# Attention with key blocks in pairs, row maxima spread over the whole pass, and the divisions split between VectorE and GpSimd

## The chip, the cores and the metric

The kernel runs on one core of a Trainium2 chip. The metric is the device time of one execution in microseconds (us). It is one program of eight stages (four layers of a mixer and a feed-forward part each); the change touches one of them, the attention of the third layer.

## The reference, cut to attention

x is (4, 48, 48, 128), so each of 4 images is a sequence of 2304 tokens; there are 4 heads of 32 channels. Queries and keys are normalised over the sequence (axis 1), not over the channels.

```python
qkv = jnp.einsum('bxyc,cf->bxyf', x, w_qkv)
q, k, v = jnp.split(qkv, 3, axis=-1)          # each to (B, 2304, 4, 32)
q = l2norm_axis1(q)
k = l2norm_axis1(k)
sim = jnp.einsum('bihd,bjhd->bhij', q, k) * 10.0
attn = jax.nn.softmax(sim, axis=-1)
out = jnp.einsum('bhij,bjhd->bhid', attn, v)
out = jnp.einsum('bxyd,dc->bxyc', out, w_out) + b_out
```

## The kernel before

**Passes.** attention() works on pairs of heads. A pass, pair_of_heads(pair, build), attends with one pair and at the same time builds the next one: packs holds, for each of two pairs, queries and keys of both heads as three stacked groups of 32 rows (high and low parts of the numbers), and row 96 holds the negated row maximum of the scores, against a row of ones on the keys' side. So the score matmul gives score minus maximum, and Exp can be applied at once. There are nine passes in order: a bare one (pair None) that only builds, seven that attend and build, three of each kind inside a loop over the images, and a last one that only attends. project_heads (the projections to q, k and v) comes between some of them, output (the last matmul and the addition to x) between others. Every block of engine programs ends in a barrier of all engines.

**An attending pass.** The 2304 query columns are six chunks (NCH) of 384 (R_ORDER), the keys 18 blocks (NT_) of 128. For each of the 6 x 18 steps, score(j) (L2187) makes two matmuls, one a head, into one of two pairs of PSUM banks; ScalarE takes Exp of both into probs (three buffers, L2233); apply(j) (L2194) multiplies probs with v, in f32, the two heads into the two column halves of the array, and adds up in bank 4. v carries columns of ones, so that bank 4 also receives the sums of the weights. TensorE's order is apply(j), score(j+2), and a chunk's score(0) and score(1) come after the last apply of the chunk before. At a chunk's end ScalarE copies bank 4 to kept (L2237), and VectorE copies the sums to inv (L2266), inverts (L2268) and multiplies into OT (L2271).

**Building.** SyncE's queue issues 12 transfers from high and qk into packs (L2291) when the pass begins. From the second chunk on, TensorE's program has maxima matmuls (L2171) between the others, three a step in steps 2 to 17 of chunks 1 to 4 and in steps 2 to 9 of chunk 5. Each writes scores of 128 queries against 384 keys to one of banks 5 to 7, and VectorE reduces it to a column of top (L2251); the matmul waits until the bank's last reduce is done. There are 216 a pass. TensorE waits for all 12 transfers (semaphore packed) before the first maximum of each of these chunks. At the end top is reduced and negated (L2255), transposed by TensorE (L2175), copied (L2257), stored to DRAM and loaded into row 96 (L2293, L2295). In the bare pass the 216 maxima matmuls and reduces follow each other alone, over three banks.

**Before the first pass** GpSimd clears rows 96 to 127 of both halves of packs and sets the row of ones (L2016, L2019), while VectorE sets v's ones, neg and inv (L2009 to L2011).

Each engine works through its own program in the order written; nothing reorders it.

## Time and profile before

| | us |
|---|---|
| median of 3 runs (lowest, highest) | 10830.53 (10821.77, 10856.01) |
| profiled execution | 10839.46 |
| its span | 10837.6 |
| busy in the span: TensorE, VectorE, ScalarE, GpSimd | 8772.7, 7070.1, 4526.0, 4157.1 |

The profile is of one execution. Engines are PE (TensorE matmuls), PEld (its weight loads), DVE (VectorE), ACT (ScalarE), POOL (GpSimd) and SP (SyncE, which issues transfers); a q behind the name is the engine's queue. L2187 is line 2187 of the kernel. A row of the timeline merges equal instructions in a row: start in us from the span's start, length, line, operation, tiles, and xN for how many. An f32 product of two heads is four matmul records: the two heads beside each other, in two passes. A matmul's end is modelled, and consecutive matmuls overlap in the rows, so that distances between starts tell more than lengths. PEclk is the granted share of TensorE's clock: 1.00 is 2.4 GHz, 0.50 is 1.2 GHz. Attention lies between about 7976 and 9850 us of the span.

### The profile page before, as it was taken

Reading aid. Unit: us, or ns where it says so; the run is one execution under the profiler, and the core shown is the slowest. Engines: PE = TensorE matmul, PEld = TensorE weight load, DVE = VectorE, ACT = ScalarE, POOL = GpSimd, SP = SyncE. Lnnn points to the kernel's source line nnn. Section 1 sums busy time; section 2 is a strip of 40 time slices with the busy share of each in tenths; the row PEclk is TensorE's granted clock in tenths of the full one; section 3 lists DMA queues with packets and bytes.
Section 4 is the critical chain, followed back from the end, with each engine's and each line's share of the span. In section 5 each row is a group of like instructions: output and inputs, shape, how many; then the busy total and the mean of one; then the engine's idle time right before and its main releaser. Section 6 shows DMA issues by size and latency. Waiting matters only on the chain. (4 is left out here: it accounts for less than half of the span.)

```text
span 10837.6 us, 132369 instructions
## 1 busy us (share of the span) xinstructions
PE 8772.7 (81%) x41708; PEld 6246.0 (58%) x41708; DVE 7070.1 (65%) x9396; ACT 4526.0 (42%) x8541; POOL 4157.1 (38%) x2789
## 2 busy tenths in 40 slices
PE   5777777778777776799999999599748989896667
PEld 2444444444444443699999999588534444443445
DVE  6999899989988998444444444311256667653446
ACT  4666566656656665222222222122313444443231
POOL 3999599969977996111111111000000000000001
PEclk8999999999999998899999999766858999998678
DMA  4555355445544554000000000210310100003000
GB/s 130 165 161 164 111 162 163 144 129 161 162 131 144 160 163 128 16 14 12 14 10 14 14 12 10 76 35 21 125 37 22 24 18 14 21 11 126 16 25 18
DMA packets 332625, 835.00 MB, mean 77 GB/s; under 512 B 36307, under 2 KB 112247, under 8 KB 318301
## 3 DMA queue, kind: packets, MB, share of 16 engines
q1 hardware_dynamic: 331940, 826.57, 25.0%
q8 instruction: 345, 5.65, 0.2%
q14 instruction: 340, 2.78, 0.1%
HBM read 758.78 MB, written 39.08 MB: 74 GB/s over the span
## 5 line engine op out<-in xcount | busy, mean ns | idle before, releaser
L754 POOL TENSOR_TENSOR ss_work<-ss_dtu,ss_ringb 128x768 f32<-128x768 f32 x1536 | 2758.0, 1819 | 251.9 <-POOLq L59 248.5
L618 PE MATMUL ss_ps<-ss_work,ss_ident 128*128 128x512 f32 (+1 forms) x6144 | 2277.8, 517 | 446.4 <-POOL ss_work L764 327.4
L618 PEld LDWEIGHTS ss_ps<-ss_work,ss_ident 128*128 128x128 f32 x6144 | 1221.5, 203 | 1222.4 <-issue 877.7
L738 DVE TENSOR_TENSOR_SCAN ss_work<-ss_ps,ss_last,ss_work 128x768 f32<-128x768 f32 x1024 | 1811.4, 1802 | 96.0 <-issue 44.5
L671 ACT ACTIVATE ss_ps<-ss_dt,ss_a_neg 128x768 f32<-128x768 f32 x1536 | 1375.9, 896 | 273.1 <-DVE ss_work L738 254.6
L1234 ACT ACTIVATE stu_XT<-cv_ps 128x384 fp32r<-128x384 f32 x768 | 377.8, 492 | 1788.8 <-DVE cv_ps L1281 1361.4
L723 DVE TENSOR_TENSOR ss_work<-ss_work,ss_ps 128x1152 f32<-128x1152 f32 x768 | 1019.9, 1328 | 1.2 <-ACT ss_ps L679 1.2
L2233 ACT ACTIVATE at_probs<-at_ps 128x768 f32<-128x768 f32 x864 | 695.6, 811 | 705.6 <-PE at_ps L2187 705.0
L2251 DVE TENSOR_REDUCE at_top<-at_ps 128x1 f32<-128x384 f32 x1728 | 878.5, 553 | 164.7 <-PE at_ps L2171 163.1
L738 DVE TENSOR_TENSOR_SCAN ss_work<-ss_ps,ss_work 128x768 f32<-128x768 f32 x512 | 879.5, 1744 | 66.5 <-POOL ss_work L754 33.3
L1275 DVE TENSOR_TENSOR stu_XT<-cv_ps,stu_XT 128x384 fp32r<-128x384 f32 x768 | 428.4, 558 | 637.6 <-ACT stu_XT L1234 615.0
L1670 POOL MEMSET c_pooled<- 128x2048 f32 x2 | 3.6, 1808 | 2110.1 <-POOLq L59 2110.1
L764 POOL TENSOR_TENSOR ss_work<-ss_work,ss_ringc 128x384 f32<-128x384 f32 x768 | 771.5, 1005 | 85.8 <-DVE ss_work L738 66.5
L2194 PE MATMUL at_ps<-at_probs,at_v 128*64 128x384 f32 x3456 | 758.5, 517 | 31.0 <-ACT at_probs L2233 28.9
L1143 POOL TENSOR_TENSOR cv_near<-cv_raw,cv_one 128x768 fp32r<-128x768 f32 (+1 forms) x32 | 46.9, 1467 | 1896.4 <-PE cv_ps L1168 1888.3
L1168 PE MATMUL cv_ps<-cv_near,stu_u_high 128*128 128x384 f32 (+2 forms) x3072 | 634.9, 296 | 0.0
L2171 PE MATMUL at_ps<-at_packs 96*128 96x384 f32 x1728 | 576.6, 411 | 31.6 <-DMA at_packs<-at_high 31.6
L1185 PE MATMUL cv_ps<-stu_XT,cv_eff_high 128*128 128x144 f32 (+3 forms) x3072 | 577.4, 282 | 0.2 <-issue 0.2
L1281 DVE TENSOR_TENSOR cv_ps<-cv_ps,cv_shared 128x384 f32<-128x384 f32 x512 | 290.0, 566 | 414.6 <-PE cv_ps L1168 414.2
L2171 PEld LDWEIGHTS at_ps<-at_packs 96*128 96x128 f32 x1728 | 336.3, 200 | 377.2 <-DVE at_top L2251 324.5
L1271 DVE TENSOR_TENSOR stu_YT<-stu_YT,cv_ps 128x384 f32<-128x384 f32 x768 | 420.5, 548 | 181.6 <-PE cv_ps L1185 174.8
L2187 PE MATMUL at_ps<-at_packs 128*128 128x384 f32 x1728 | 482.3, 365 | 54.2 <-PEq L59 44.2
(546 smaller groups left out, 15466.7 us busy)
## 6 DMA issues: line engine op xcount, KB each, us to landing
ss_ringb<-scan_rows SPq DMA_DIRECT2D x768, 384.0 KB, 3.6
ss_ringc<-scan_rows SPq DMA_DIRECT2D x768, 384.0 KB, 3.7
c_w<-in_l_ffn_w SPq DMA_DIRECT2D x64, 1024.0 KB, 7.3
at_packs<-at_high SPq DMA_DIRECT2D x64, 288.0 KB, 5.5
cv_raw<-in_l_ffn_phi_odd SPq DMA_DIRECT2D x16, 576.5 KB, 3.7
cv_raw<-in_l_ffn_phi_even SPq DMA_DIRECT2D x16, 576.0 KB, 4.2
ffa_rows<-rows SPq DMA_DIRECT2D x16, 576.0 KB, 6.2
at_packs<-at_qk SPq DMA_DIRECT2D x32, 288.0 KB, 5.5
```

The source lines that it names most:

```text
L618: return pe.matmul(acc[:, d * WIN + a:d * WIN + e], ident[:, :], weighed[:, t % DEEP, d, a:e], start=n == 0 and e - a == 512, stop=n == NS ...
L671: act.activation(decay[d], dt[:, i % 2, d, :], ACT.Exp, scale=a_neg[:, SECTIONS[i][0], d, n:n + 1]).then_inc(s["decayed"], 1)
L723: dve.tensor_tensor(weighed[:, t % DEEP, :, 0:SPLIT], hid[:, t % DEEP, :, 0:SPLIT], bc(spread_c[:, None, :], [P, D2, SPLIT]), ALU.mult).th ...
L738: dve.tensor_tensor_scan(hid[:, t % DEEP, d, ::step], decay[d][:, ::step], drive[:, t % DEEP, d, ::step], start, ALU.mult, ALU.add).then_i ...
L754: pool.tensor_tensor(drive[:, t % DEEP, d, :], dtu[:, t // NST % 2, d, :], ringb[:, t % RING, :], ALU.mult).then_inc(s["driven"], 1)
L764: pool.tensor_tensor(weighed[:, t % DEEP, :, SPLIT:WIN], hid[:, t % DEEP, :, SPLIT:WIN], bc(ringc[:, t % RING, None, SPLIT:WIN], [P, D2, W ...
L1168: ins = pe.matmul(ps[:, bank, off:CW], blocks(a, g, parity), taps[kind][f][:, ::-1][:, from_:from_ + CW - off], start=start and g == 0 and ...
L1185: ins = pe.matmul(ps[:, 4 + c, lo:hi], (eff_high, eff_low)[a][:, kind, seg, :], (uk_high, uk_low)[f][:, (NCW * n + c) % SLOTS, lo:hi], sta ...
L2171: pe.matmul(ps_bank(ps, 5 + u % 3)[:, 0:R], packs[0:96, build, QUERIES, h, tile * P:(tile + 1) * P], packs[0:96, build, KEYS, h, u * R:(u ...
L2194: ins = pe.matmul(acc[64 * h:64 * h + 64, 0:R], v[:, j, 2 * pair + h, :, :].rearrange("p a d -> p (a d)"), probs[:, j % 3, h, :], start=j ...
L2233: act.activation(probs[:, j % 3, :, :], ps[:, 2 * (j % 2):2 * (j % 2) + 2, 0:R], ACT.Exp).then_inc(s["weighed"], 1)
L2251: dve.tensor_reduce(top[:, bass.ds(tile + h * NT_, 1), u], ps_bank(ps, 5 + u % 3)[:, 0:R], AX.X, ALU.max).then_inc(s["reduced"], 1)
```

## The change

probs has four buffers instead of three. TensorE goes through the 108 steps of a pass as 54 pairs, without regard to chunks: in pair p it makes the scores of steps 2p+2 and 2p+3 (of the next chunk too, where one ends), with the maxima that are due between them, and then the products of steps 2p and 2p+1. The maxima are in one list of 216, spread evenly over pairs 2 to 50 by maxima_due, four or five a pair; the wait for the 12 transfers stands before the first of them. ScalarE copies a chunk's result after the second exp of the next chunk. For the first five chunks GpSimd makes the copies of the sums and the multiplications, and VectorE the reciprocal in two halves, in two successive pairs; for the last chunk VectorE does all. In the bare pass the maxima are made in threes: three matmuls into three banks, one reduce over 3 x 384 columns, two sets of banks. The clearing of packs is split: VectorE does one half, GpSimd the other.

```diff
--- before.py
+++ after.py
@@ -1990,7 +1990,7 @@
-        probs = sb("probs", [P, 3, 2, R_ORDER])
+        probs = sb("probs", [P, 4, 2, R_ORDER])
@@ -1998,11 +1998,11 @@
-        xb = probs[:, :, :, :].rearrange("p a h r -> p (a h r)")
+        xb = probs[:, 0:3, :, :].rearrange("p a h r -> p (a h r)")
         ps = ctx.enter_context(nc.psum_tensor("at_ps", [P, 8, 512], F32))
-        c0 = Signals(nc, "at0", "cleared")
+        c0 = Signals(nc, "at0", "cleared filled")
         with nc.Block() as block:
             @block.vector
             def _(dve):
@@ -2010,18 +2010,20 @@
                 dve.memset(neg[:, :], 0.0)
                 dve.memset(inv[:, :], 1.0)
+                dve.memset(packs[96:P, 0, :, :, :].bitcast(F32), 0.0).then_inc(c0["cleared"], 1)
+                dve.wait_ge(c0["cleared"], 1)
+                dve.memset(packs[96:97, 0, KEYS, :, :].bitcast(F32), 1.0)
             @block.gpsimd
             def _(pool):
...
+                pool.memset(packs[96:P, 1, :, :, :].bitcast(F32), 0.0).then_inc(c0["filled"], 1)
+                pool.wait_ge(c0["filled"], 1)
+                pool.memset(packs[96:97, 1, KEYS, :, :].bitcast(F32), 1.0)
         c0.end()
         s1 = Signals(nc, "at1", "loaded made kept own squared rooted")
         s3 = Signals(nc, "at3", "packed mmade reduced negated turned copied stored placed "
-                                "scored weighed used kept divided own")
+                                "scored weighed used kept sums_ready inverted divided own")
@@ -2136,6 +2138,19 @@
+def maxima_groups():
+    return [(t, h, u) for t in range(NT_) for h in range(2) for u in range(NCH)]
+def maxima_due(p):
+    pairs = NCH * NT_ // 2
+    first, last = 2, pairs - 3
+    total = 2 * NT_ * NCH
+    return 0 if p < first else min(total, (p - first + 1) * total // (last - first))
 def pair_of_heads(nc, s, pair, build, vv):
@@ -2145,140 +2160,160 @@
     R = R_ORDER
     acc = ps_bank(ps, 4)
     STEPS = 2 * (len(ROWS[QUERIES]) + len(ROWS[KEYS]))
+    BLOCKS = NCH * NT_
+    GROUPS = maxima_groups()
...
+    def turned_sums(eng):
+        for h in range(2):
+            ins = eng.tensor_copy(inv[64 * h:64 * h + DH, :], kept[64 * h + DH:64 * h + 2 * DH, :])
+        return ins
+    def rows_of(c, h):
+        at = (2 * pair + h) * DH
+        return OT[at:at + DH, c * R:(c + 1) * R], kept[64 * h:64 * h + DH, :], inv[64 * h:64 * h + DH, :]
     with nc.Block() as block:
         @block.tensor
         def _(pe):
...
+            def maxima(g):
+                tile, h, u = GROUPS[g]
+                if g == 0:
+                    pe.wait_ge(s["packed"], 16 * STEPS)
+                at_least(pe, s["reduced"], g - 2)
+                pe.matmul(ps_bank(ps, 5 + g % 3)[:, 0:R], packs[0:96, build, QUERIES, h, tile * P:(tile + 1) * P],
+                          packs[0:96, build, KEYS, h, u * R:(u + 1) * R], start=True, stop=True).then_inc(s["mmade"], 1)
+            def maxima_of_three(g):
+                tile, h, u = GROUPS[3 * g]
+                at_least(pe, s["reduced"], g - 1)
+                for n in range(3):
+                    ins = pe.matmul(ps_bank(ps, 3 * (g % 2) + n)[:, 0:R], packs[0:96, build, QUERIES, h, tile * P:(tile + 1) * P],
+                                    packs[0:96, build, KEYS, h, (u + n) * R:(u + n + 1) * R], start=True, stop=True)
+                ins.then_inc(s["mmade"], 1)
...
+            def score(n):
+                c, j = n // NT_, n % NT_
+                at_least(pe, s["weighed"], n - 1)
+                for h in range(2):
+                    ins = pe.matmul(ps_bank(ps, 2 * (n % 2) + h)[:, 0:R], packs[:, pair, KEYS, h, j * P:(j + 1) * P],
+                                    packs[:, pair, QUERIES, h, c * R:(c + 1) * R], start=True, stop=True)
+                ins.then_inc(s["scored"], 1)
+            def apply(n):
+                c, j = n // NT_, n % NT_
+                pe.wait_ge(s["weighed"], n + 1)
+                if j == 0:
+                    at_least(pe, s["kept"], c)
+                for h in range(2):
+                    ins = pe.matmul(acc[64 * h:64 * h + 64, 0:R], v[:, j, 2 * pair + h, :, :].rearrange("p a d -> p (a d)"), probs[:, n % 4, h, :],
+                                    start=j == 0, stop=j == NT_ - 1, skip_group_check=True)
+                ins.then_inc(s["used"], 1)
+            if pair is None:
+                pe.wait_ge(s["packed"], 16 * STEPS)
+                for g in range(len(GROUPS) // 3):
+                    maxima_of_three(g)
+                turn()
+            else:
                 score(0)
                 score(1)
...
+                for p in range(BLOCKS // 2):
+                    due = range(maxima_due(p - 1), maxima_due(p)) if build is not None else []
+                    for g in due[0:2]:
+                        maxima(g)
+                    if p + 1 < BLOCKS // 2:
+                        score(2 * p + 2)
+                    for g in due[2:3]:
+                        maxima(g)
+                    if p + 1 < BLOCKS // 2:
+                        score(2 * p + 3)
+                    for g in due[3:]:
+                        maxima(g)
+                    apply(2 * p)
+                    apply(2 * p + 1)
+                    if build is not None and p == BLOCKS // 2 - 3:
                         turn()
...
         @block.scalar
         def _(act):
...
+            def weigh(n):
+                act.wait_ge(s["scored"], n + 1)
+                at_least(act, s["used"], n - 3)
+                act.activation(probs[:, n % 4, :, :], ps[:, 2 * (n % 2):2 * (n % 2) + 2, 0:R], ACT.Exp).then_inc(s["weighed"], 1)
+            def keep(c):
+                act.wait_ge(s["used"], (c + 1) * NT_)
                 at_least(act, s["divided"], c)
                 act.activation(kept[:, :], acc[:, 0:R], ACT.Copy).then_inc(s["kept"], 1)
             if pair is not None:
-                chunks(act, weigh)
+                for n in range(BLOCKS):
+                    weigh(n)
+                    if n > NT_ and n % NT_ == 1:
+                        keep(n // NT_ - 1)
+                keep(NCH - 1)
         @block.vector
         def _(dve):
...
+            def reduce(g):
+                tile, h, u = GROUPS[g]
                 dve.wait_ge(s["mmade"], g + 1)
...
+                dve.tensor_reduce(top[:, bass.ds(tile + h * NT_, 1), u], ps_bank(ps, 5 + g % 3)[:, 0:R], AX.X, ALU.max).then_inc(s["reduced"], 1)
+            def reduce_three(g):
+                tile, h, u = GROUPS[3 * g]
+                dve.wait_ge(s["mmade"], g + 1)
+                dve.tensor_reduce(top[:, bass.ds(tile + h * NT_, 1), u // 3], ps[:, 3 * (g % 2):3 * (g % 2) + 3, 0:R], AX.XY, ALU.max).then_inc(s["reduced"], 1)
+            def negate(parts):
+                dve.wait_ge(s["reduced"], 2 * NT_ * parts)
+                dve.tensor_reduce(neg[:, 0:2 * NT_], top[:, :, 0:parts], AX.X, ALU.max, negate=True).then_inc(s["negated"], 1)
                 dve.wait_ge(s["turned"], 1)
                 dve.tensor_copy(topT[:, :].bitcast(F32R), ps_bank(ps, 5)[:, 0:P]).then_inc(s["copied"], 1)
...
+            def half_inverted(c, half):
+                dve.wait_ge(s["sums_ready"], c + 1)
+                part = inv[:, half * R // 2:(half + 1) * R // 2]
+                dve.reciprocal(part, part).then_inc(s["inverted"], 1)
+            if pair is None:
+                for g in range(len(GROUPS) // 3):
+                    reduce_three(g)
+                negate(NCH // 3)
+            else:
+                for p in range(BLOCKS // 2):
+                    for g in range(maxima_due(p - 1), maxima_due(p)) if build is not None else []:
+                        reduce(g)
+                    if p >= NT_ // 2 and p % (NT_ // 2) in (1, 2):
+                        half_inverted(p // (NT_ // 2) - 1, p % (NT_ // 2) - 1)
+                if build is not None:
+                    negate(NCH)
+                ch = Chain(dve, s["own"])
+                dve.wait_ge(s["kept"], NCH)
+                ch.link(turned_sums(dve))
                 ch.link(dve.reciprocal(inv[:, :], inv[:, :]))
                 for h in range(2):
-                    at = (2 * pair + h) * DH
-                    ins = dve.tensor_tensor(OT[at:at + DH, c * R:(c + 1) * R], kept[64 * h:64 * h + DH, :], inv[64 * h:64 * h + DH, :], ALU.mult)
+                    ins = dve.tensor_tensor(*rows_of(NCH - 1, h), ALU.mult)
                 ins.then_inc(s["divided"], 1)
+        @block.gpsimd
+        def _(pool):
             if pair is not None:
...
+                for c in range(NCH - 1):
+                    pool.wait_ge(s["kept"], c + 1)
+                    turned_sums(pool).then_inc(s["sums_ready"], 1)
+                    pool.wait_ge(s["inverted"], 2 * (c + 1))
                     for h in range(2):
...
+                        ins = pool.tensor_tensor(*rows_of(c, h), ALU.mult)
+                    ins.then_inc(s["divided"], 1)
         @block.sync
         def _(sp):
```

## Rows read from the trace of the kernel before

**Rows 1.** The page, costliest groups: busy and mean | idle before, and its releaser
```profile
L2171 PE MATMUL at_ps<-at_packs 96*128 96x384 f32 x1728 | 576.6, 411 | 31.6 <-DMA at_packs<-at_high 31.6
```

**Rows 2.** Windows: stretch, length, busy us of PE, PEld, DVE, ACT, POOL; PEclk, DMA, GB/s
```profile
7982.30:8006.30 24.00, 0.00 (x0) 0.00 (x0) 2.50 (x3) 0.00 (x0) 23.30 (x4) 0.50 0.00 0
...
8057.50:8158.80 101.30, 100.50 (x216) 62.03 (x216) 100.46 (x217) 0.00 (x0) 0.00 (x0) 0.50 0.00 0
8165.90:8356.40 190.50, 186.53 (x865) 92.95 (x865) 133.61 (x243) 90.67 (x115) 0.00 (x0) 0.98 0.09 20
...
8359.60:8368.30 8.70, 0.00 (x0) 0.00 (x0) 1.68 (x3) 0.00 (x0) 0.00 (x0) 0.50 0.39 136
8393.60:8400.40 6.80, 6.28 (x16) 2.73 (x16) 0.00 (x0) 3.59 (x4) 0.00 (x0) 0.50 0.86 174
...
9673.00:9823.70 150.70, 146.60 (x648) 54.72 (x648) 21.78 (x25) 89.39 (x113) 0.00 (x0) 0.99 0.00 1
```

**Rows 3.** Timeline, TensorE, a block without maxima: start, us, engine, line, operation
```profile
8181.24 0.61 PE L2187 MATMUL at_ps<-at_packs 128*128 128x384 f32 x2
8181.78 0.87 PE L2194 MATMUL at_ps<-at_probs,at_v 128*64 128x384 f32 x4
```

**Rows 4.** Timeline, a block with three maxima, TensorE and then VectorE
```profile
8240.11 0.87 PE L2194 MATMUL at_ps<-at_probs,at_v 128*64 128x384 f32 x4
8240.91 0.44 PE L2171 MATMUL at_ps<-at_packs 96*128 96x384 f32 x1
8241.19 0.52 PE L2187 MATMUL at_ps<-at_packs 128*128 128x384 f32 x2
8241.54 0.52 PE L2171 MATMUL at_ps<-at_packs 96*128 96x384 f32 x2
8241.99 0.87 PE L2194 MATMUL at_ps<-at_probs,at_v 128*64 128x384 f32 x4
...
8241.39 1.55 DVE L2251 TENSOR_REDUCE at_top<-at_ps 128x1 f32<-128x384 f32 x3 [0.32 <-PE at_ps L2171]
```

**Rows 5.** Timeline of TensorE, the first instructions of the first attending pass
```profile
8165.92 1.62 PE L2187 MATMUL at_ps<-at_packs 128*128 128x384 f32 x4 [6.24 <-PEq L59]
8167.97 1.55 PE L2194 MATMUL at_ps<-at_probs,at_v 128*64 128x384 f32 x4 [0.43 <-ACT at_probs L2233]
8169.45 1.01 PE L2187 MATMUL at_ps<-at_packs 128*128 128x384 f32 x2
```

**Rows 6.** DMA issues (page: last column us to landing), SyncE and ScalarE at two passes
```profile
at_packs<-at_high SPq DMA_DIRECT2D x64, 288.0 KB, 5.5
...
8179.77 1.41 SPq L2291 DMA_DIRECT2D at_packs<-at_high  x1
...
8356.35 0.49 ACT L2237 ACTIVATE at_kept<-at_ps 128x384 f32<-128x384 f32 x1 [0.96 <-PE at_ps L2194]
...
8614.64 1.40 SPq L2291 DMA_DIRECT2D at_packs<-at_high  x1
...
8795.59 0.49 ACT L2237 ACTIVATE at_kept<-at_ps 128x384 f32<-128x384 f32 x1 [0.96 <-PE at_ps L2194]
```

**Rows 7.** Timeline at a chunk's end, TensorE
```profile
8225.76 0.95 PE L2171 MATMUL at_ps<-at_packs 96*128 96x384 f32 x3
```

**Rows 8.** Reciprocals of VectorE by line, busy us and mean ns
```profile
L2268 DVE RECIPROCAL at_inv<-at_inv 128x384 f32<-128x384 f32 x6 | 15.3, 2553 | 0.2
...
L111 DVE RECIPROCAL at_ln_rstd<-at_ln_std 128x72 f32<-128x72 f32 x1 | 0.6, 603 | 0.4 <-ACT at_ln_std L121 0.4
```

**Rows 9.** Operations of another stage, from the page
```profile
L764 POOL TENSOR_TENSOR ss_work<-ss_work,ss_ringc 128x384 f32<-128x384 f32 x768 | 771.5, 1005 | 85.8 <-DVE ss_work L738 66.5
...
L723 DVE TENSOR_TENSOR ss_work<-ss_work,ss_ps 128x1152 f32<-128x1152 f32 x768 | 1019.9, 1328 | 1.2 <-ACT ss_ps L679 1.2
```

**Rows 10.** Memsets of GpSimd and of VectorE by line
```profile
L2016 POOL MEMSET at_packs<- 32x9216 f32 x2 | 15.5, 7773 | 273.5 <-POOLq L59 273.5
...
L320 DVE MEMSET ss_dtr<- 32x2304 f32 x1 | 2.0, 1978 | 0.5 <-issue 0.5
```

More of the change, by code:

```diff
@@ L2166, in _ @@
         def _(pe):
-            def maxima(group):
-                g, tile, h, u = group
-                pe.wait_ge(s["reduced"], g + 1)
-                pe.matmul(ps_bank(ps, 5 + u % 3)[:, 0:R], packs[0:96, build, QUERIES, h, tile * P:(tile + 1) * P], packs[0:96, build, KEYS, h, u * R:(u + 1) * R], start=True, stop=True).then_inc(s["mmade"], 1)
+            def maxima(g):
[12 more added lines that the diff above has]
+                ins.then_inc(s["mmade"], 1)
             def turn():
@@ L2198, in attend @@
+            if pair is None:
[4 more added lines that the diff above has]
+            else:
                 score(0)
                 score(1)
-                at_least(pe, s["kept"], c)
-                for j in range(NT_):
-                    apply(j)
-                    at = 3 * (j - 2)
-                    for group in groups[at:at + 1] if j >= 2 else []:
-                        maxima(group)
-                    if j + 2 < NT_:
-                        score(j + 2)
-                    for group in groups[at + 1:at + 3] if j >= 2 else []:
-                        maxima(group)
-                    if build is not None and c == NCH - 1 and j == 12:
-                        turn()
@@ L2215, in _ @@
-            if pair is not None:
-                chunks(pe, attend)
-            else:
-                pe.wait_ge(s["packed"], 16 * STEPS)
-                for tile in range(NT_):
-                    for h in range(2):
-                        for u in range(NCH):
-                            maxima(((2 * tile + h) * NCH + u, tile, h, u))
-                turn()
+                for p in range(BLOCKS // 2):
[13 more added lines that the diff above has]
+                    if build is not None and p == BLOCKS // 2 - 3:
+                        turn()
@@ L2239, in _ @@
             if pair is not None:
-                chunks(act, weigh)
+                for n in range(BLOCKS):
[3 more added lines that the diff above has]
+                keep(NCH - 1)
         @block.vector
         def _(dve):
-            ch = Chain(dve, s["own"])
-            dve.sem_inc(s["reduced"], 3)
-            def reduce(group):
-                g, tile, h, u = group
+            def reduce(g):
+                tile, h, u = GROUPS[g]
@@ L2256, in negate @@
                 dve.wait_ge(s["turned"], 1)
                 dve.tensor_copy(topT[:, :].bitcast(F32R), ps_bank(ps, 5)[:, 0:P]).then_inc(s["copied"], 1)
-            def divide(c):
-                for group in maxima_groups(c):
-                    reduce(group)
-                if build is not None and c == NCH - 1:
-                    negate()
-                dve.wait_ge(s["kept"], c + 1)
-                for h in range(2):
-                    ins = dve.tensor_copy(inv[64 * h:64 * h + DH, :], kept[64 * h + DH:64 * h + 2 * DH, :])
-                ch.link(ins)
+            def half_inverted(c, half):
+                dve.wait_ge(s["sums_ready"], c + 1)
+                part = inv[:, half * R // 2:(half + 1) * R // 2]
+                dve.reciprocal(part, part).then_inc(s["inverted"], 1)
@@ L2268, in divide @@
                 ch.link(dve.reciprocal(inv[:, :], inv[:, :]))
                 for h in range(2):
-                    at = (2 * pair + h) * DH
-                    ins = dve.tensor_tensor(OT[at:at + DH, c * R:(c + 1) * R], kept[64 * h:64 * h + DH, :], inv[64 * h:64 * h + DH, :], ALU.mult)
+                    ins = dve.tensor_tensor(*rows_of(NCH - 1, h), ALU.mult)
                 ins.then_inc(s["divided"], 1)
+        @block.gpsimd
+        def _(pool):
             if pair is not None:
-                chunks(dve, divide)
-            else:
-                for tile in range(NT_):
+                for c in range(NCH - 1):
+                    pool.wait_ge(s["kept"], c + 1)
+                    turned_sums(pool).then_inc(s["sums_ready"], 1)
+                    pool.wait_ge(s["inverted"], 2 * (c + 1))
@@ L2278, in _ @@
                     for h in range(2):
-                        for u in range(NCH):
-                            reduce(((2 * tile + h) * NCH + u, tile, h, u))
-                negate()
+                        ins = pool.tensor_tensor(*rows_of(c, h), ALU.mult)
+                    ins.then_inc(s["divided"], 1)
         @block.sync
```

41 lines of the change are left out of this document (removed).

## The prediction

> **What bounds the kernel now.** I read the page first, then busy time and clock by stretch, then the attention passes instruction by instruction, and last the transfers that feed them. It puts the weight of the kernel elsewhere: attention takes some 1850 of 10,838 us, and nothing outside it is edited. So only attention is worked out. On the page, see one line: the maxima matmuls waited 31.6 us for a transfer into at_packs [rows 1]. That is the first, bare pass, the only place where maxima are asked for as soon as a pass begins.
>
> By stretch [rows 2], an attending pass that also builds the next pair's maxima is 190.5 us long with TensorE busy in 186.5, VectorE in 133.6 and ScalarE in 90.7; the last pass, which builds nothing, has 146.6 of 150.7. TensorE bounds both. In the bare pass VectorE is busy 100.5 of 101.3 us, and TensorE stands at 0.50 of its clock (1.2 GHz).
>
> The steps show what TensorE's time is made of. Without maxima [rows 3] a block is two score matmuls and four product records (two heads side by side, two passes each), and repeats every 1.34 us: the scores start 0.54 us before the products, and the products 0.80 after that give way to scores. With three maxima [rows 4] it is 1.87 us from one product start to the next (8240.11 to 8241.99, with the rounding of a row). Narrow matmuls in a row start 0.177 apart (8241.19 to 8241.54 is two of them). A second product pass starts 0.87 - 0.49 = 0.37 us after the first. With these, a block of 2 scores and a product would be 2 x 0.177 + 2 x 0.373 = 1.10; it takes 1.34. So 0.24 us is paid for changing over from scores to products and back, and the same 0.24 is left with five narrow matmuls: 1.87 - 5 x 0.177 - 0.746. No exp is late: ScalarE is idle for half of the pass.
>
> **Pairs of blocks.** 108 blocks a pass become 54 pairs, each 4 x 0.177 + 4 x 0.373 + 0.24 = 2.44 us without maxima. One changeover in two goes: 54 x 0.24 = 13.0 us a pass. What no row shows is a product right behind another block's product. Low end 0.373 a pass, as inside a block; high end a full drain, which by the score row and the latest product end is about 0.2 us each, 54 x 0.2 = 11 us a pass. I take the low one, since the second pass inside a block writes the same bank with new weights and pays 0.373. The Trainium skill, "TensorEngine Tiling (Array Packing)", Tiling Modes, says that the array drains when its tiling mode changes, not when only the tile does. Two products share one mode; by that rule the low end holds and the rival of a drain below loses weight; the 0.24 above agrees with it.
>
> **Next chunk's scores ahead.** Now the first product of a chunk waits for kept, behind the last product and a 0.49 copy. A building pass of 72 x 1.87 + 36 x 1.34 = 182.9 takes 190.5; the last 108 x 1.34 = 144.7 takes 150.7. The rest, 7.6 and 6.0, is five chunk ends and the start at the low clock. In the new order four scores (0.8 us with the changeover) stand between a chunk's last product and the next one, and the copy begins 0.05 us after the product and takes 0.5: hidden, with 0.2 to spare. With four probs buffers neither exp nor product waits: a pair's two exps are 1.6 us in 2.44.
>
> Last pass: start at the low clock and first pair 5.3 us (four score matmuls 1.6 us, a wait for exp, four more, and a product at 1.48 for 0.80 until the clock rises [rows 5]), then 52 pairs x 2.44 = 126.9, the last without scores 1.5: 133.7 against 150.7. **Gain 17.0 us.**
>
> **Maxima spread over the pass: the wait.** The seven building passes ask for maxima from the third pair (maxima_due is 0 for p below 2, then about 4.4 a pair to p = 50). The first of them still waits for all 12 transfers into packs, and TensorE's queue holds everything behind it: scores, products, hence ScalarE and VectorE. Third pair begins at 5.3 + 2.4 and a little, 8 to 9 us after TensorE's start. SyncE issues the last transfer at 8179.77, the pass having begun at 8165.92 [rows 5, 6], and such a transfer lands 5.5 us after its issue: 19.4 us in. Now that is hidden, as no maximum is asked for in the first chunk (26 us long). **TensorE will stand still for about 11 us**; in the two passes behind output, where SyncE starts 3.5 us before TensorE, for 7.
>
> So a building pass is best counted from that landing to its end. Before: 8185.3 to the last copy's start at 8356.35, 171.1, in the pass shown; 175.5 in the third (last issue 8614.64, copy 8795.59) [rows 6]. Of the seven, four are of the first kind (171.4 mean), two of the second (175.4), and the seventh is 169.0: 1205.4 us together. After, by terms:
> - 49 pairs x 2.44 and 216 maxima x 0.177: 157.8.
> - two pairs without maxima 4.9, the last pair 1.5, the turn 0.2: 6.6.
> - Bank waits. Three banks take the maxima. A reduce starts 0.38 after its matmul, the next 0.47 behind it, it ends after 0.55, and a matmul held by it starts 0.15 after that end [rows 4, 7] (three in a row take 0.95 us where 0.80 is due, as the last was held for its bank). In a pair with five maxima (216 - 4 x 49 = 20 of them) the fifth is wanted at 8 x 0.177 = 1.42 and its bank is free at 0.38 + 0.47 + 0.55 + 0.15 = 1.55: 20 x 0.14 = 2.8.
> - Half reciprocals. The rows for 384 and 72 columns, 2553 and 603 ns [rows 8], give 1.35 us for 192. Two pairs in each of five chunks have it behind their reduces. Worked pair by pair it makes the next pair's maxima wait 0.2 to 0.5: 2.7 in all. Bounds: nothing, if the backlog is gone by the next pair; 0.5 each, 5.
> - Clock. From 3.2 us after a pass's end the clock was 0.50 with TensorE idle; a restarted TensorE had 0.50 for 6.8 us in the second pass [rows 2], and 4 to 8 in the others. The stall is long enough for that. At the low clock a product goes by in 1.48 for 0.80 (8167.97 to 8169.45), and four score matmuls take 1.62 for 0.97 [rows 5], so 5.5 us of it lose 2.4.
> Sum 172.3, times seven 1206.1, against 1205.4. **Gain 0.** Without the transfer wait a pass would be 5.3 + 2.4 + 157.8 + 6.6 + 5.5 = 177.6 against 190.5: the spreading takes back what pairs bring.
>
> Behind it: the last product to the pass's end (copy, turn, reciprocal, multiply of the last chunk) stays on VectorE, as now. The turn comes 4 us before the last product instead of 6; the two small transfers behind it need 3.6, and VectorE's tail is 5, so they stay covered.
>
> **Division shared with GpSimd.** GpSimd is idle here [rows 2]; its two copies of 32x384 have no row; a 128x384 two-input op of its own is 1.0 us [rows 9], which I take as the upper end, nothing as the lower. They start when kept is done, and VectorE asks for the result a pair later, 4.8 us on. Hidden; the copies may cost 2.4 us each before TensorE feels it. The multiplies have a chunk's time.
>
> **Bare pass in threes of banks.** 72 reduces of 1152 columns. 216 now take 100.5, 0.465 each, of which successive ones overlap by 0.09. VectorE's 1152 columns with a PSUM input take 1.33 in another stage [rows 9], so 1.24 each, 89.3 in all. But two sets of three banks go round a ring: three matmuls with their handshakes, at the low clock 1.43 (1.62 for four less one spacing of 0.32, and 0.13 for the waits), then the reduce, 1.33, for two groups: 1.38 a group, 99.4. The clock was 0.50 through 101 us of this pass [rows 2] with one matmul in 0.465; the new pass would be as dense. I take 1 us gained; 11 if the clock rises.
>
> **Memsets.** GpSimd's four take 23.3 of the 24.0 us before the first loads [rows 2, 10]. Split: VectorE has its 2.5 and 9216 columns at the 1.98 per 2304 of its own row, 7.9, and half of that, 4.0: 14.5. Gain 8.2 (bounds 11.6, GpSimd's own half, and 0 if they share a port). The Trainium skill, "GPSIMD Engine Reference", Key points, warns that GpSimd and a VectorE instruction in a two-port mode contend for memory. Here VectorE's three memsets (2304, 384 and 128 columns) took 2.50 us beside GpSimd's [rows 2], against 2.42 at the rate of the lone one at L320 [rows 10]; the trace speaks against a loss. By that rule, if it held for memsets, the 8.2 would shrink towards 0.
>
> **Sum.** 17.0 - 0.7 (called 0 above) + 1 + 8.2, about 25.5 us. The profiled execution took 10,839.5 (its span 10,837.6 and 1.9 around it), 0.08% over the median 10,830.5 of the runs; I put the difference on the median: 10,805, 0.24% less. A measurement here can tell about 0.3% (32 us).
>
> **Rivals.**
> 1. VectorE's backlog is harmless: no bank or reciprocal wait, 7 x 5.5 = 38 us, perhaps the clock of the bare pass too (10): 10,757 to 10,790, I say 10,780. For it: VectorE is busy for 70% only. Against: a row in which the fourth matmul was held [rows 7].
> 2. The transfers don't hold the third pair. Then 7 x (190.5 - 177.6) = 90 more: 10,715. Nothing speaks for it but that landings could come earlier; the wait is on all twelve.
> 3. **Slower:** a product drains before the next block's product. 0.2 us at 54 places in 8 passes, 86 us: 10,891. For: no row shows the seam. It decides from 0.06 us a seam, where the gain is gone. Against: the second pass in a block.
> 4. VectorE's queue is worse than worked: contention of GpSimd's copies with its reduces, or reciprocals in pairs of five that each hold TensorE 1 us instead of 0.3: 7 x 10 x 0.7 = 49: 10,854.
>
> **How the numbers follow.** Forecast 0.52 (own range 10,788 to 10,828), rival 1 0.20, rival 2 0.07, rival 3 0.09, rival 4 0.12. Faster by over 0.3% is below 10,798: rivals 1 and 2 nearly whole, 0.26, and 0.11 of the forecast's: 0.37. Slower, above 10,863: rival 3 and 0.03 of rival 4: 0.12. Within: 0.51. The range 10,770 to 10,855 leaves out rivals 2 and 3 and the edges of 1 and 4.
>
> **What would show it.** TensorE idle for 7 to 11 us at the first maxima matmul in each building pass, released by a transfer into at_packs, then about 6 us at 0.50 of the clock; pairs of 2.44 us in the last pass, 3.15 and 3.46 with four and five maxima; building passes again near 190, the last 134; the bare pass near 100 at clock 0.50; GpSimd's memsets 11.7 us. Building passes near 178 would refute the wait; pairs of 2.6 or more the changeover.

## The result and the profile after

| | before | after |
|---|---|---|
| median (lowest to highest), us | 10836.2 (10821.8 to 10856.0), 4 runs | 10750.5 (10737.0 to 10765.3), 4 runs |
| ratio | | 0.9919, 95% interval 0.9905 to 0.9934 |
| span of the profiled execution, us | 10837.6 | 10753.0 |

The change makes the kernel 0.8% faster, some 86 us. I had forecast 25 us, within the noise, and a range down to 10,770: the time lies outside it, on the fast side.

The page of the kernel after, its span, busy TensorE, and the line that answers to [rows 1]. Columns of the last: busy, mean ns | idle before it.

```profile
span 10753.0 us, 132231 instructions
PE 8643.1 (80%) x41708; PEld 6312.2 (59%) x41708; DVE 6950.3 (65%) x9134; ACT 4479.2 (42%) x8541; POOL 4262.7 (40%) x2947
...
L2187 PE MATMUL at_ps<-at_packs 96*128 96x384 f32 x1512 | 497.6, 376 | 63.0 <-DMA at_packs<-at_high 62.9
```

The maxima matmuls of the seven building passes now wait 62.9 us for a transfer in all: about 10 us (9.9 to 10.7) in five of them and 6.0 in the two behind output. Before, they waited for none. The 31.6 us of [rows 1] was the bare pass's own wait; after the change that matmul stands at another line (L2194), its wait is as long as it was, and it is not in the 62.9.

Windows of the kernel after, columns as in [rows 2]: the clearing of packs, the bare pass, the first attending pass and, within it, the stall and what follows, and the last pass.

```profile
7977.00:7994.80 17.80, 0.00 (x0) 0.00 (x0) 14.13 (x5) 0.00 (x0) 11.70 (x2) 0.50 0.00 0
8046.90:8148.20 101.30, 93.05 (x216) 59.20 (x216) 94.49 (x73) 0.00 (x0) 0.00 (x0) 0.50 0.00 0
8155.10:8338.50 183.40, 172.51 (x865) 102.29 (x865) 116.84 (x228) 85.40 (x114) 14.95 (x20) 0.96 0.10 20
8163.90:8174.20 10.30, 0.01 (x1) 0.00 (x0) 0.00 (x0) 0.00 (x0) 0.00 (x0) 0.71 0.91 187
8174.30:8178.40 4.10, 4.10 (x12) 2.92 (x14) 2.14 (x4) 1.62 (x2) 0.00 (x0) 0.50 0.00 0
9610.60:9740.80 130.20, 129.89 (x648) 62.98 (x648) 12.82 (x10) 84.13 (x113) 14.91 (x20) 0.97 0.00 1
```

The first building pass is 183.4 us instead of 190.5, the last pass 130.2 instead of 150.7, and the bare pass as long as before at the same 0.50 of the clock. From first score to last product, the seven building passes together went from 1333.8 to 1279.5 us (54.3 less), the last from 150.7 to 130.2 (20.5), the clearing from 23.4 to 17.7 (5.7), the bare pass with its tail from 108.3 to 108.3. The gaps between passes took 2.7 more, which I can't explain, and 5.3 us of the difference of the two spans lie before attention, where nothing was edited: variation between executions.

TensorE at the third pair of the first attending pass (timeline: start, us, line, operation, count, idle before and its releaser):

```profile
8162.77 1.14 PE L2216 MATMUL at_ps<-at_probs,at_v 128*64 128x384 f32 x6
8174.27 1.01 PE L2187 MATMUL at_ps<-at_packs 96*128 96x384 f32 x2 [10.37 <-DMA at_packs<-at_high]
```

That is the forecast stall: 10.37 us, released by the last transfer into at_packs. It stands in every building pass: in the five where TensorE and SyncE start together the landing is 19.0 to 19.3 us after TensorE's first score, in the two behind output 15.3. The window from 8163.9 shows no engine busy, with the transfers at 0.91 of the DMA engines, and the one from 8174.3 has TensorE at 0.50 for 4.1 us. All that was close to the forecast (11 us and 7 us of standing still, then 5.5 us at the low clock). What was not is the pair itself. TensorE in the last pass:

```profile
9650.50 0.97 PE L2206 MATMUL at_ps<-at_packs 128*128 128x384 f32 x4
9651.40 1.51 PE L2216 MATMUL at_ps<-at_probs,at_v 128*64 128x384 f32 x8
9652.84 0.97 PE L2206 MATMUL at_ps<-at_packs 128*128 128x384 f32 x4
9653.74 0.87 PE L2216 MATMUL at_ps<-at_probs,at_v 128*64 128x384 f32 x4
```

Compare [rows 3]. Two products follow each other in 1.51 us; the first pass of the run is 0.373 as before, and (1.51 - 0.49 - 0.37) / 2 = 0.32 separates the later ones. From scores to scores it is 1.44 us for two products, against 2 x 0.80. The whole pair repeats every 2.34 us (9650.50 to 9652.84, or 9651.40 to 9653.74), where I had 2.44.

A pair with five maxima, TensorE and then VectorE:

```profile
8229.90 0.62 PE L2187 MATMUL at_ps<-at_packs 96*128 96x384 f32 x2
8230.36 0.52 PE L2206 MATMUL at_ps<-at_packs 128*128 128x384 f32 x2
8230.72 0.34 PE L2187 MATMUL at_ps<-at_packs 96*128 96x384 f32 x1
8230.90 0.51 PE L2206 MATMUL at_ps<-at_packs 128*128 128x384 f32 x2
8231.25 0.65 PE L2187 MATMUL at_ps<-at_packs 96*128 96x384 f32 x2
8231.83 1.51 PE L2216 MATMUL at_ps<-at_probs,at_v 128*64 128x384 f32 x8
8233.27 0.62 PE L2187 MATMUL at_ps<-at_packs 96*128 96x384 f32 x2
```

```profile
8230.38 2.42 DVE L2269 TENSOR_REDUCE at_top<-at_ps 128x1 f32<-128x384 f32 x5 [1.10 <-PE at_ps L2187]
8232.72 1.34 DVE L2285 RECIPROCAL at_inv<-at_inv 128x192 f32<-128x192 f32 x1
8233.97 1.88 DVE L2269 TENSOR_REDUCE at_top<-at_ps 128x1 f32<-128x384 f32 x4
```

Such a pair is 3.37 us (8229.90 to 8233.27), one with four is 3.05: the fifth costs 0.32, its own 0.177 and 0.14 of waiting for its bank, as worked. Behind it VectorE's half reciprocal of 1.34 us delays the next pair's first reduce by 0.22, and the four matmuls of that pair don't notice (8233.27 to 8236.34, 3.07).

### The profile page after: what moved, and what is told of

Same layout as the page of the kernel before. It is cut to its first block and busy times, and to the rows that moved or that the text cites. A ratio compares the mean times of both kernels' runs of the same rounds, so it can differ in the third digit from the quotient of the medians.

```text
span 10753.0 us, 132231 instructions
## 1 busy us (share of the span) xinstructions
PE 8643.1 (80%) x41708; PEld 6312.2 (59%) x41708; DVE 6950.3 (65%) x9134; ACT 4479.2 (42%) x8541; POOL 4262.7 (40%) x2947
## 5 line engine op out<-in xcount | busy, mean ns | idle before, releaser
L2269 DVE TENSOR_REDUCE at_top<-at_ps 128x1 f32<-128x384 f32 x1512 | 730.9, 547 | 439.4 <-PE at_ps L2187 439.4
L2250 ACT ACTIVATE at_probs<-at_ps 128x768 f32<-128x768 f32 x864 | 653.9, 807 | 706.4 <-PE at_ps L2206 705.1
L2216 PE MATMUL at_ps<-at_probs,at_v 128*64 128x384 f32 x3456 | 668.7, 510 | 0.0
L2172 POOL COPY at_inv<-at_kept 32x384 f32<-32x384 f32 x80 | 39.9, 499 | 1296.2 <-ACT at_kept L2255 1294.5
L2187 PE MATMUL at_ps<-at_packs 96*128 96x384 f32 x1512 | 497.6, 376 | 63.0 <-DMA at_packs<-at_high 62.9
L1168 PEld LDWEIGHTS cv_ps<-cv_near,stu_u_high 128*128 128x128 f32 x3072 | 515.8, 189 | 0.0
L2206 PE MATMUL at_ps<-at_packs 128*128 128x384 f32 x1728 | 458.4, 356 | 58.3 <-PEq L59 44.4
```

Source lines behind the costliest of these rows:

```text
L1168: ins = pe.matmul(ps[:, bank, off:CW], blocks(a, g, parity), taps[kind][f][:, ::-1][:, from_:from_ + CW - off], start=start and g == 0 and ...
L2187: pe.matmul(ps_bank(ps, 5 + g % 3)[:, 0:R], packs[0:96, build, QUERIES, h, tile * P:(tile + 1) * P], packs[0:96, build, KEYS, h, u * R:(u ...
L2216: ins = pe.matmul(acc[64 * h:64 * h + 64, 0:R], v[:, j, 2 * pair + h, :, :].rearrange("p a d -> p (a d)"), probs[:, n % 4, h, :], start=j ...
L2250: act.activation(probs[:, n % 4, :, :], ps[:, 2 * (n % 2):2 * (n % 2) + 2, 0:R], ACT.Exp).then_inc(s["weighed"], 1)
L2269: dve.tensor_reduce(top[:, bass.ds(tile + h * NT_, 1), u], ps_bank(ps, 5 + g % 3)[:, 0:R], AX.X, ALU.max).then_inc(s["reduced"], 1)
```

## The experiments

Each is the changed kernel with one edit, unless it says more. "After" is 10,750.5.

**Maxima later.**

```diff
-    first, last = 2, pairs - 3
+    first, last = 7, pairs - 3
```

> The changed kernel with one number changed: the maxima begin with pair 7 instead of pair 2 and are spread over 44 pairs. Theory (the third pair waits for the last of the 12 transfers): TensorE stood still for 10.4 us in five of the building passes and 6.5 us in the two behind output, and ran about 4 us at 0.50 of the clock after it. Pair 7 is reached 20.4 us after TensorE's start (8.7 for two pairs, 5 x 2.34), behind the landing at 19.2, so the stall goes. Against it, 40 instead of 20 pairs have five maxima, each 0.14 us late: 2.8 us. A building pass of 183.5 becomes 171 to 173, the two others 174 to 175; together 55 to 75 us less than the changed kernel, some 10,685. Rival (the idle time is only moved, as VectorE is then the limit in the denser pairs): a pass stays above 180 and the whole within 15 us of the changed kernel.

Measured: 10,701.1 (10,687.5 to 10,711.8), ratio to before 0.9875 (0.9858 to 0.9891): 49 us below after. TensorE at the first maxima:

```profile
8187.74 0.97 PE L2206 MATMUL at_ps<-at_packs 128*128 128x384 f32 x4
8188.64 1.51 PE L2216 MATMUL at_ps<-at_probs,at_v 128*64 128x384 f32 x8
8190.08 0.62 PE L2187 MATMUL at_ps<-at_packs 96*128 96x384 f32 x2
```

No idle time before 8190.08, and no low clock. The passes are 174.2 to 175.3 us, the two behind output among them; by the sum of all eight, 1351.5 against 1409.7, 58 us. By the medians the gain is below the 55 to 75 us that I wrote, by the passes just inside. The wait was real, but moving it gives back less than it cost. A building pass became 8.1 us shorter on average, where the stall was 6.0 to 10.7 us and the low clock behind it took about 2 more: 40 pairs instead of 20 now have five maxima, 0.14 us late each, and one that follows a pair with a half reciprocal takes 3.52 us instead of 3.37 (nine pairs a pass instead of two).

**Products out of their pairs.**

```diff
                     if p + 1 < BLOCKS // 2:
                         score(2 * p + 2)
-                    for g in due[2:3]:
+                    apply(2 * p)
+                    for g in due[2:]:
                         maxima(g)
                     if p + 1 < BLOCKS // 2:
                         score(2 * p + 3)
-                    for g in due[3:]:
-                        maxima(g)
-                    apply(2 * p)
                     apply(2 * p + 1)
```

> The changed kernel with the products taken out of their pairs: score(2p+2), product(2p), score(2p+3), product(2p+1); everything else stays. Theory (a run of products saves a changeover of 0.24 us and also lets the second product's passes go at 0.322 instead of 0.373): pairs without maxima go from 2.34 back to 2.67 us, the last pass from 130 to 148, the building passes by 15 to 17 each (the fives lose their bank wait of 0.14): 120 to 140 us more in all, near 10,880, slower than before the change, because the transfer wait stays. Rival (my prediction's price, 13 us a pass; the rest of the measured gain came from the even spreading and the fourth probs buffer): 2.58 us a pair and at most 104 us more.

Measured: 10,875.6 (10,865.6 to 10,882.9), ratio to before 1.0039 (1.0024 to 1.0053). That is 125 us above after, and slower than before the change. TensorE in the last pass:

```profile
9769.74 0.87 PE L2216 MATMUL at_ps<-at_probs,at_v 128*64 128x384 f32 x4
9770.53 0.62 PE L2206 MATMUL at_ps<-at_packs 128*128 128x384 f32 x2
9771.08 0.87 PE L2216 MATMUL at_ps<-at_probs,at_v 128*64 128x384 f32 x4
```

1.34 us a block again, 2.69 a pair, the last pass 149.5, and a building pass 14.3 us longer than after. The rival with 104 us is refuted: pairs bring 0.35 us each, in the terms of my prediction 0.24 for the changeover and 0.10 for the second product. All the other parts together, without pairs, cost 40 us net; the stall alone is more than that, 61 us at the seven third pairs of this run.

**Blocks in threes in the last pass.** The edits of e8_late_and_warm, the last experiment below, are also in it, so the last pass is judged by itself.

```diff
-        probs = sb("probs", [P, 4, 2, R_ORDER])
+        probs = sb("probs", [P, 6, 2, R_ORDER])
...
+            elif build is None:
+                for n in range(3):
+                    score(n)
+                for t in range(BLOCKS // 3):
+                    for n in range(3 * t + 3, min(3 * t + 6, BLOCKS)):
+                        score(n)
+                    for n in range(3 * t, 3 * t + 3):
+                        apply(n)
...
```

> e8_late_and_warm, and in the last pass, which builds nothing, the blocks in threes: six scores (banks 0 and 1, 2 and 3, 5 and 6), then three products, with six probs buffers. It tests the price of a product in a run. Theory (a changeover costs about 0.25, and each pass of a product behind the first starts 0.322 later): a run of three takes 0.281 + 4 x 0.175 + 0.269 + 0.373 + 4 x 0.322 + 0.42 = 3.33 us, 36 of them 120 against 54 x 2.34 = 126: the last pass is 6 us shorter. Rival (my prediction's price of 0.373 a pass and 0.24 a changeover): 6 x 0.177 + 6 x 0.373 + 0.24 = 3.54 us a run, 127, no gain.

Measured: 10,678.4 (10,670.0 to 10,690.1), ratio 0.9858 (0.9842 to 0.9874), indistinguishable as a whole from the kernel without threes (10,677.5). But the last pass is 122.9 us against 129.0. TensorE:

```profile
9600.59 2.16 PE L2226 MATMUL at_ps<-at_probs,at_v 128*64 128x384 f32 x12
9602.67 1.34 PE L2216 MATMUL at_ps<-at_packs 128*128 128x384 f32 x6
9603.94 1.83 PE L2226 MATMUL at_ps<-at_probs,at_v 128*64 128x384 f32 x10
```

Three products in 2.16 us: 2.16 - 0.49 - 0.37 = 1.30 for four spacings, 0.325 each. A run repeats in 3.35 us (9600.59 to 9603.94); worked by 0.322 it is 3.33, by my prediction's price 3.54. So the price that failed is settled by a run of another length. One, two and three blocks a run repeat in 1.34, 2.34 and 3.35 us: each block adds two narrow matmuls at 0.175 and two product passes at 0.322, 1.0 us, and each run costs 0.35 once for going over and back. At about 0.35 us a pair, that is what e2_singles lost.

**Order at a chunk's end undone.**

```diff
+                    closes = p % (NT_ // 2) == NT_ // 2 - 1
...
-                    if p + 1 < BLOCKS // 2:
+                    if p + 1 < BLOCKS // 2 and not closes:
                         score(2 * p + 2)
...
                     apply(2 * p + 1)
+                    if p + 1 < BLOCKS // 2 and closes:
+                        score(2 * p + 2)
+                        score(2 * p + 3)
...
+                    if n and n % NT_ == 0:
+                        keep(n // NT_ - 1)
                     weigh(n)
-                    if n > NT_ and n % NT_ == 1:
-                        keep(n // NT_ - 1)
```

> The changed kernel with the order at a chunk's end undone: in the last pair of a chunk TensorE makes the products first and then the next chunk's scores, and ScalarE copies the chunk's result before the next chunk's exps. Theory (the scores ahead hide the first exps and the copy): a chunk's end costs again what it did before, 0.7 us in the last pass and some 0.9 in a building pass, five ends in eight passes: 28 to 40 us more than the changed kernel, about 10,785. Rival (with four probs buffers and pairs the end was hidden anyway): under 8 us more.

Measured: 10,794.1 (10,778.0 to 10,812.4), ratio 0.9964 (0.9954 to 0.9975), 44 us above after. TensorE at a chunk's end in the last pass:

```profile
9684.98 2.80 PE L2216 MATMUL at_ps<-at_probs,at_v 128*64 128x384 f32 x16
9687.71 0.96 PE L2206 MATMUL at_ps<-at_packs 128*128 128x384 f32 x4
9689.23 1.32 PE L2206 MATMUL at_ps<-at_packs 128*128 128x384 f32 x4 [0.55 <-ACT at_probs L2254]
9690.47 1.51 PE L2216 MATMUL at_ps<-at_probs,at_v 128*64 128x384 f32 x8
```

TensorE waits 0.55 us for the exp before the third block's scores, and it is 1.24 us from the first of those four matmuls to the next product, 0.90 in the pair shown above. There is one changeover less, as two pairs' products form one run. Together the two pairs take 5.49 us (9684.98 to 9690.47) instead of 4.68, 0.8 an end; the last pass is 3.2 us longer, as its start took 0.8 less. A building pass is 6.0 longer on average, 1.2 an end. The theory holds, and the whole cost more than the 28 to 40 us that I gave, through the building passes. At one of their ends the rows show 0.30 us of waiting for a bank, where four maxima follow each other without scores between them, and 0.21 for the exp.

**Division on VectorE alone.**

```diff
-                    if p >= NT_ // 2 and p % (NT_ // 2) in (1, 2):
-                        half_inverted(p // (NT_ // 2) - 1, p % (NT_ // 2) - 1)
+                    if p >= NT_ // 2 and p % (NT_ // 2) == 1:
+                        divide(p // (NT_ // 2) - 1)
...
```

> The changed kernel with the division undone: VectorE does copies, the whole reciprocal and the multiplies of each chunk in one go, in the second pair of the next chunk; GpSimd does nothing. Theory (VectorE's queue holds the maxima's banks): the piece of 4.4 us instead of two of 1.3 leaves the next pair's reduces late by about 3 us, and TensorE waits for the banks: 2 to 3 us at each of five places in seven passes, 70 to 105 us more. Rival (VectorE has 30% idle time and catches up): under 15 us more.

Measured: 10,923.5 (10,913.4 to 10,936.3), ratio 1.0085 (1.0069 to 1.0102), 173 us above after. TensorE, and then VectorE, at one of the places:

```profile
8206.60 1.15 PE L2187 MATMUL at_ps<-at_packs 96*128 96x384 f32 x2 [3.00 <-DVE at_top L2269]
8207.68 2.67 PE L2216 MATMUL at_ps<-at_probs,at_v 128*64 128x384 f32 x8
8210.28 0.62 PE L2187 MATMUL at_ps<-at_packs 96*128 96x384 f32 x2
...
8201.51 0.71 DVE L2172 COPY at_inv<-at_kept 32x384 f32<-32x384 f32 x2
8202.26 2.55 DVE L2297 RECIPROCAL at_inv<-at_inv 128x384 f32<-128x384 f32 x1
8204.85 1.11 DVE L2299 TENSOR_TENSOR at_OT<-at_kept,at_inv 32x384 f32<-32x384 f32 x2
8205.99 2.42 DVE L2269 TENSOR_REDUCE at_top<-at_ps 128x1 f32<-128x384 f32 x5
```

VectorE is away from the reduces for 4.4 us, TensorE stands for 3.00 and holds its scores and products too. From product to product the pair took 7.0 us and the next 4.2, 4.8 more than their due, and a pass is 25 us longer. The rival is refuted, but the stall is not all of the cost. Behind it TensorE had 0.54 of its clock (8206.60 to 8210.28; 1.00 before and after), and the two products took 2.60 us instead of 1.44. The seven building passes have 35 such places, with 3.0 to 3.2 us of standing still in each. At three of them the clock stayed at 1.00, and they cost 3.4 us; at the 32 others it fell to 0.50 for a while, and they cost 4.8 to 6.2. So about 119 us (35 x 3.4) are the backlog on VectorE, for which I had allowed 70 to 105, and some 50 are the clock, which I had left out. In the last pass, without maxima, the same edit costs nothing (129.2 us). Before the change the division began in two steps without maxima, [rows 3] rather than [rows 4]. So with maxima in every pair the division can't stay in one piece on VectorE. The edit took away GpSimd's share and the halving of the reciprocal together; all of it on VectorE in smaller pieces was not run.

**What sets the bare pass.** With threes, TensorE fills one set of three banks while VectorE reduces the other, and each waits for the other's signal: that is the ring of the texts below. Three kernels. One matmul and one reduce at a time, as before:

```diff
-                for g in range(len(GROUPS) // 3):
-                    maxima_of_three(g)
+                for g in range(len(GROUPS)):
+                    maxima(g)
...
```

> The changed kernel with the bare pass as before, one matmul and one reduce at a time over three banks. To be read in the trace, from the pass's first matmul to the next pass's: theory (at 0.50 of the clock threes gain nothing, as the ring of two bank sets takes 1.39 us a group against 3 x 0.465): within 1 us of the changed kernel's 108.25. Rival (threes save the start of two reduces in three): 5 to 10 us more.

Measured: 108.12 us from the first matmul to the next pass, against 108.25. Threes bring nothing at this clock. The one execution took 10,744.5.

Every matmul of the bare pass twice:

```diff
-                for n in range(3):
+                for n in [0, 0, 1, 1, 2, 2]:
```

> The changed kernel with every matmul of the bare pass made twice, into the same bank. It tells what sets the bare pass's 1.39 us a group. Theory (a ring of two bank sets at the low clock: matmuls, handshake, reduce): if the denser TensorE is granted 1.00, six matmuls take 1.06 us and VectorE's reduce of 1.24 alone sets the pace, 89 us for the pass, 11 us less than now. If the clock stays at 0.50 the ring grows by 3 x 0.32 = 0.96 for two groups: 1.87 a group, 135 us, 35 more. Rival (VectorE's reduce is what takes 1.39): no difference at either clock as long as six matmuls fit.

Measured: 10,756.9 (10,751.6 to 10,758.5), ratio 0.9929 (0.9912 to 0.9946), the same as after within the noise. Windows and VectorE:

```profile
8051.30:8055.20 3.90, 3.90 (x14) 3.83 (x14) 2.78 (x3) 0.00 (x0) 0.00 (x0) 0.50 0.00 0
8055.30:8148.00 92.70, 87.14 (x402) 66.64 (x400) 88.33 (x67) 0.00 (x0) 0.00 (x0) 1.00 0.00 1
...
8080.05 5.42 DVE L2274 TENSOR_REDUCE at_top<-at_ps 128x1 f32<-128x1152 f32 x4
```

The clock rose to 1.00 some 6 us after the first matmul, and the reduces come no faster: the window of 92.7 us holds 67 of them, 1.38 each, and from the first matmul to the next pass it is 110.1 us instead of 108.25. My 89 us was a mistake in the expectation: six matmuls at 2.4 GHz last as long as three at 1.2, so the ring was the same. This run alone does not rule out the rival; the next one does.

Extra matmuls outside of the ring, together with the later maxima:

```diff
                 ins.then_inc(s["mmade"], 1)
+                for n in range(3):
+                    pe.matmul(ps_bank(ps, 6)[:, 0:R], packs[0:96, build, QUERIES, h, tile * P:(tile + 1) * P],
+                              packs[0:96, build, KEYS, h, (u + n) * R:(u + n + 1) * R], start=True, stop=True)
```

> Maxima from pair 7 on, as in e1_late_maxima, and in the bare pass three more matmuls behind each group, into bank 6, which nothing reads. In e6_bare_double, where the doubled matmuls were part of the ring, the clock rose to 1.00 in the bare pass and the group still took 1.39 us, as six matmuls at 2.4 GHz last as long as three at 1.2. Theory (ring and clock): here the extra ones stand outside the ring, three matmuls, handshake and reduce make 2.4 us for two groups, so VectorE alone sets the pace at 1.27 us: the bare pass gets 7 to 9 us shorter, the whole 8 us below e1_late_maxima, near 10,693. Rival (the reduce over three banks takes 1.39 by itself): no gain. If the extra matmuls don't raise the clock, they cost up to 30 us.

Measured: 10,677.5 (10,665.4 to 10,685.0), ratio 0.9856 (0.984 to 0.9872), the fastest together with the one in threes, and 24 us below the kernel with late maxima alone. The trace gives 7.5 of that to this edit (bare pass 100.8 us against 108.35). Of the 26.8 us between the two profiled spans 17.9 lie before attention, where both kernels are the same. Windows and VectorE:

```profile
8048.00:8135.00 87.00, 86.51 (x413) 68.45 (x411) 87.00 (x70) 0.00 (x0) 0.00 (x0) 1.00 0.00 1
...
8078.66 6.40 DVE L2277 TENSOR_REDUCE at_top<-at_ps 128x1 f32<-128x1152 f32 x5
```

VectorE is busy 87.00 of 87.00 us, reduces 1.27 apart ((6.40 - 1.34) / 4), so the rival's 1.39 for the reduce itself is refuted. The matmuls that nobody reads pay for themselves through the clock.

## Why the prediction was wrong, step by step

- **The changeover and the product in a run: the step that failed.** I took 0.373 a pass as the low end, "as inside a block". In the kernel before, every second product pass is the first after a changeover; there was no row of a third. The first spacing after a changeover carries 0.05 us that belongs to the changeover, the others are 0.322. So the low end of my bounds was no end, and it was the value I took. The mechanism, one changeover saved a pair, was right; the term 4 x 0.373 was mis-sized, and 2.44 us a pair measured 2.34. 0.10 us a pair is 5.4 us a pass, 43 us of the 60 by which I was off; 17 more are the half reciprocals below, and 7 lie outside attention, where nothing was edited. Against these stand some 8 us that the memsets, the start of the last pass, the gaps and the bare pass fell short.
- **Last pass**: 133.7 forecast, 130.2 measured: 5.4 less by that term, 1.9 more at the start, where the clock was low for 8.2 us (4.1 before; in e1_late_maxima, whose last pass has the same program, 5.0, and the pass took 128.7).
- **Chunk ends hidden**: right; 0.8 to 1.2 us an end, as the kernel with the old order showed.
- **The wait for the transfers**: right in place, releaser and, nearly, size (9.9 to 10.7 for "about 11", 6.0 for 7). With later maxima it went.
- **From landing to end of a building pass**: 172.3 forecast, 164.7 measured. Products about 5; the half reciprocals cost 0.3 instead of 2.7 (two pairs of 3.51 against 3.37), since a reduce behind a reciprocal starts before that one's end (8233.97 against 8234.06) and pairs of four have slack; the clock 1.9 instead of 2.4 in the first pass (4.9 us for a pair of 3.05), and 2.8 in the two behind output. The bank wait of the fives was right to 0.01 us.
- **GpSimd**: right that it is hidden. Two copies take 1.04 us, the two multiplies 2.04:

```profile
8227.52 1.04 POOL L2172 COPY at_inv<-at_kept 32x384 f32<-32x384 f32 x2 [16.69 <-ACT at_kept L2255]
8237.20 2.04 POOL L2315 TENSOR_TENSOR at_OT<-at_kept,at_inv 32x384 f32<-32x384 f32 x2 [8.64 <-DVE at_inv L2285]
```

- **Bare pass**: 0.1 us gained for "1", clock and ring as forecast. VectorE reduces in twos, 2.78 us for two groups:

```profile
8078.81 2.62 DVE L2274 TENSOR_REDUCE at_top<-at_ps 128x1 f32<-128x1152 f32 x2 [0.15 <-PE at_ps L2194]
8081.59 2.62 DVE L2274 TENSOR_REDUCE at_top<-at_ps 128x1 f32<-128x1152 f32 x2 [0.15 <-PE at_ps L2194]
```

- **Memsets**: 5.7 us gained for 8.2. My 8.2 does not follow from my terms, which give 23.3 - 14.5 = 8.8. The instructions were as priced, but VectorE waited 1.96 and 1.02 us before its two (the gaps in brackets), which I had not counted:

```profile
7979.74 0.38 DVE L2011 MEMSET at_inv<- 128x384 f32 x1
7982.08 7.74 DVE L2013 MEMSET at_packs<- 32x9216 f32 x1 [1.96 <-issue]
7990.84 3.90 DVE L2015 MEMSET at_packs<- 1x4608 f32 x1 [1.02 <-issue]
```

- **Rivals**: the first (no backlog in VectorE) was right for the reciprocals, wrong for the fives, which wait. Its lowest time, 10,757, is nearest to what was measured, but by luck: it rests on banks that nobody waits for and on a faster bare pass, and neither came. Its 38 us also give 10,767, not the 10,780 that I wrote. The second is refuted by the stall. The third, a drain between products, is refuted with the opposite sign: that seam is cheaper than the one inside a block. The fourth did not come; the kernel that divides on VectorE alone shows what a longer piece in VectorE's queue costs.

The sum of my terms said that spreading the maxima from the third pair eats what pairs bring. It eats half of what they could bring: a building pass was 190.5 on average before, is 182.8 after, and 174.7 with the later maxima.

## What to carry to other kernels

A cost per instruction read off a trace is the cost at its place in the pattern; where a change makes a pattern that the trace does not hold (a third pass in a row), the nearest row is not the lower bound, and splitting changeover from steady spacing must wait for a run long enough. When work is spread evenly over a loop, look at the first item: it brings its wait for the inputs to the front of an in-order queue, and here a later start gave 49 us. And an engine with 30% idle time can still stop another one, if its long instruction falls between short ones that free buffers; where the stopped one is TensorE, look at the granted clock behind the stall before pricing it.

## What the runs showed of the hardware

- Products of two heads in the two column halves, f32, 384 columns: the first spacing after full-width matmuls 0.373 us, every later one 0.322; going over to scores and back costs 0.35 us in all at 2.4 GHz, the 0.05 of that first spacing with it (after, e9_threes_last).
- TensorE kept 1.2 GHz through 101 us of three matmuls in 1.39 us (after). With six a group it was busy without a break at 1.2 GHz (3.90 of 3.90 us), and it had 2.4 GHz within 7 us of its first matmul (e6_bare_double).
- Behind a stall of 3.0 to 3.2 us in a busy TensorE the granted clock fell to 0.50 at 32 of 35 places and stayed at 1.00 at three; a place cost 4.8 to 6.2 us with the fall and 3.4 without (e4_divide_dve).
- VectorE's maximum over 3 x 384 PSUM columns takes 1.34 us and repeats at 1.27; three of 384 repeat at 0.465 each, 1.40.
- GpSimd copies 32 x 384 in 0.5 us and multiplies them in 1.0, and VectorE's reduces beside it were not longer (0.541 us mean for those that overlap one of its instructions, 0.548 for the others).
